# Moving the steps of the output chain and the empty places in the list that orders the ring of the third stage

## The chip, the cores and the metric

The kernel runs on one core of one Trainium2 chip. The metric is device time in microseconds (us), lower is better; the time stated for a kernel is the median of its runs. The engines are called TensorE (PE), VectorE (DVE), ScalarE (ACT), GpSimd (POOL) and SyncE (SP), as in the profile.

## The reference

Two cross-attentions and two feed-forward layers, each on a layer norm and added to x, for 4 batches of 256 rows of width 512. The context has 1601 rows per batch. The part that matters is the second attention (third stage of the kernel) and the last layer:

```python
def _L1_xattn_ref(latents, context, Wq, Wk, Wv, Wo):      # H, KV, HD = 16, 4, 96; G = 4
    hidden = jnp.concatenate([context, latents], axis=1)  # 1857 rows
    q = (latents @ Wq.T).reshape(b, q_len, H, HD)
    k = (hidden @ Wk.T).reshape(b, s_len, KV, HD)
    v = (hidden @ Wv.T).reshape(b, s_len, KV, HD)
...
    scores = jnp.einsum('bkgqd,bksd->bkgqs', q, k) * scale
    attn = jax.nn.softmax(scores.astype(jnp.float32), axis=-1).astype(q.dtype)
    out = jnp.einsum('bkgqs,bksd->bkgqd', attn, v)
...
    return out @ Wo.T
...
x = x + _L1_xattn_ref(_layernorm(x, axis=-1), ctx_4096, L1_xattn_Wq, ...)
x = x + _L1_ffn_ref(_layernorm(x, axis=-1), L1_ffn_W, L1_ffn_b, L1_ffn_A, L1_ffn_Bmat, L1_ffn_LiMEs)
```

## The kernel before

Three stages run one after the other. The first two make the keys, values and queries of the second attention and put them into DRAM. The third, `grouped_attention`, starts at about 1015 us of the span and is the only one that the change touches.

**Steps and tiles.** The third stage has 16 steps `s`, one for each batch and key head. A step covers 4 query heads x 256 rows = 1024 columns and goes over 15 key tiles `kt` of 128 keys (the last has 65). For each tile TensorE computes the scores (`scores`, lines 1502 to 1504, two halves of 512 columns, three products each, since every operand is split in a high and a low part), ScalarE takes the exponential twice (`probs`, lines 1604 and 1607), GpSimd subtracts the two to get the low part (line 1417), and TensorE multiplies with the values (`values`, lines 1522, 1523, 1525, two halves of three products). TensorE does the scores one tile ahead: in the loop over `kt` it does `scores(s, kt + 1)` and then `values(s, kt)`. The banks of the scores go round three by three.

**The ring.** Beside this, the step has a list of other work, `beside(s)`, whose entries are called places here and counted from 0. TensorE takes one place after the first half of the scores, one after the second, one after the first half of the values and one after the second: four a tile up to tile 11, two in tiles 12 and 13. `None` is an empty place. The entries are: 32 `max`, the products (line 1435) that give the maxima of the scores for the next step `s + 1`, each read by VectorE's reduction (line 1690); four `stacked`, nine products each (line 1458), which multiply the output of the step before, `s - 1`, with the output weights, read by VectorE (line 1698); in steps 5, 9 and 13 also the last layer of the batch that is complete (`turn`, `h`, `z`, `h8`, `dl`); and three entries that only VectorE acts on (`OWN`). For TensorE these three are empty places. The items share three banks (`RB = 3`): TensorE may write ring item n only when VectorE has read item n - 3. VectorE reads them in the order of the list, and does its own entries where they stand.

**The output chain.** When step `s` ends, its output and the sums of its exponentials have to be turned into rows, divided, stacked and multiplied with the output weights. This happens in step `s + 1`, through DRAM:
- ScalarE copies the output out (line 1652) and issues sums<-o (line 1611), right after the first tile's exponentials of the new step;
- VectorE inverts the sums: own entry `invert` (line 1720);
- ScalarE sends the inverted sums to DRAM, `send_parts` (line 1615), and spreads them over the partitions, `spread_parts` (line 1619), which waits for the sent values to land;
- VectorE multiplies: own entry `normal` (line 1724), which waits for the spread;
- ScalarE copies the product out, `send_o` (line 1623), and back in stacked form, `stack_o` (line 1628), and rounds it, `stacked_hi` (line 1635);
- VectorE subtracts the rounded part: own entry `low` (line 1728);
- TensorE can then do the `stacked` items; the first waits for both parts.

ScalarE does its five steps behind the exponentials of fixed tiles, and each of them waits, on ScalarE, for what it needs; the exponentials of the next tile stand behind it. The steps named with DMAs are issued from ScalarE's queue; SyncE's queue loads keys, queries, values and weights of later steps.

**Layer norm.** In steps 5, 9 and 13 VectorE starts with the layer norm of the batch that is complete, 19 small operations, between which `fill(1)` takes seven places of the list, one at a time.

Of the kernel before, what the change touches and what calls it, by code (L numbers as in the profile page):

```python
# [1193 lines left out]
def grouped_attention(nc, A, ident, negid, ps, ln, home, q_scr, k_scr, v_scr, x_scr, wo_scr, sum_scr, o_scr, w1T, out):  # L1194
# [16 lines left out]
    with ExitStack() as ctx:  # L1211
# [3 lines left out]
        def sem(name):  # L1215
            return ctx.enter_context(nc.semaphore(name))
# [62 lines left out]
        step, w_mix, mix_ones = sem("dve_step1"), sem("w_mixture"), sem("mixture_ones")  # L1279
# [6 lines left out]
        def bank(i, n=BANK):  # L1286
            return ps[:, i * BANK:i * BANK + n]
# [5 lines left out]
        def beside(s):  # L1293
            maxima = [("max", s + 1, i) for i in range(NI)] if s + 1 < S else []
            if s == 0:
                return [None] * 12 + maxima
            if s == S:
                return [("sum", s - 1, 0)] + [("out", s - 1, i) for i in range(TT * G)]
            e = (s - 1) // KV1 - 1 if s % KV1 == 1 else -1
            later = [("turn", e, 0), ("turn", e, 1), ("h", e, 0), ("h", e, 1), ("z", e, 0), ("h8", e, 0), ("dl", e, 0)] \  # L1300
                if e >= 0 else [None] * 7
            most = maxima or [None] * NI
            own = [(kind, s - 1, 0) for kind in ("invert", "normal", "low")]
            order = most[:6] + own[:1] + most[6:14] + later[:2] + own[1:2] + most[14:19] + later[2:3] + most[19:23] + later[3:4] + most[23:26] + later[4:6] + \
                most[26:28] + later[6:] + [None, None] + own[2:] + [None]
            for i in range(NO):
                order += [("stacked", s - 1, i), most[28 + i]]
            return order
# [10 lines left out]
        for s in range(S + 1):  # L1319
            for item in beside(s) + (last_batch() if s == S else []):  # L1320
                if item and item[0] not in OWN:
                    ring[item] = len(ring)
# [98 lines left out]
        def _(pe):  # L1421
            def ring_item(kind, a, i):
# [4 lines left out]
                if kind == "max":  # L1427
                    if i == 0:
                        pe.wait_ge(qh_in[a % 3], loads(a, 3))
                        pe.wait_ge(kh_in[a % 3], loads(a, 3))  # L1430
                        if a == 1:
                            pe.wait_ge(ones, 4)
                    j, ch = i // len(cuts), i % len(cuts)
                    k0, _, k = cuts[ch]
                    mm = pe.matmul(at[:, 0:k], qh[a % 3][0:HD1, j * P:(j + 1) * P], kh[a % 3][0:HD1, k0:k0 + k],  # L1435
                                   start=True, stop=True)
# [93 lines left out]
            for s in range(S):  # L1530
                if s == 1:
                    pe.wait_ge(w_small, 48)
                items = iter(beside(s))

                def fill():
                    item = next(items, None)
                    if item and item[0] not in OWN:
                        ring_item(*item)

                if s == 0:  # L1540
                    scores(0, 0, lambda: None)
                for kt in range(KT):
                    if kt + 1 < KT:
                        scores(s, kt + 1, fill)
                        fill()
                    elif s + 1 < S:
                        scores(s + 1, 0, lambda: None)
                    if s + 1 < S and kt == KT - 2:
                        max_rows(s + 1)
                    late = kt > KT - 4  # L1550
                    values(s, kt, (lambda: None) if late else fill)
                    if not late:
                        fill()
                assert next(items, None) is None
            for item in beside(S) + last_batch():
                ring_item(*item)
# [29 lines left out]
        def _(act):  # L1586
# [9 lines left out]
            def probs(s, kt):  # L1596
                n = s * KT + kt
                if n >= 2:
                    act.wait_ge(av_mm, n - 1)
                for half in range(2):  # L1600
                    src = bank((2 * n + half) % SB)[0:keys[kt], :]
                    cols = slice(half * BANK, (half + 1) * BANK)
                    act.wait_ge(s_mm, 2 * n + half + 1)
                    act.activation(ph[0:keys[kt], n % 2, cols], src, ACT.Exp, scale=S1).then_inc(phi, 1)  # L1604
                    if 2 * n + half >= 2:
                        act.wait_ge(plo, 2 * n + half - 1)
                    act.activation(pf[0:keys[kt], half, :], src, ACT.Exp, scale=S1).then_inc(exp_done, 1)  # L1607

            def send_sums(s):
                act.wait_ge(o_done, 2 * s + 2)  # L1610
                act.dma_start(sums[:, :], o[HD1:HD1 + 1, :].rearrange("o (j m) -> o j m", j=QT)).then_inc(sum_in, 16)
# [26 lines left out]
            for s in range(S):  # L1638
                for kt in range(KT):
                    if kt:  # L1640
                        probs(s, kt)
                    if s:
                        step = {2: send_parts, 3: spread_parts, 6: send_o, 7: stack_o, 9: stacked_hi}.get(kt)
                        if step:
                            step(s - 1)
                if s + 1 < S:
                    probs(s + 1, 0)
                act.wait_ge(av_mm, (s + 1) * KT)
                if s:
                    act.wait_ge(o_out, 16 * s)  # L1650
                for half in range(2):
                    act.copy(o[0:HD1 + 1, half * BANK:(half + 1) * BANK], bank(OB + half)[0:HD1 + 1, :]).then_inc(o_done, 1)  # L1652
                send_sums(s)
# [184 lines left out]
```

## Time and profile before

| | us |
|---|---|
| median of 3 runs | 1986.28 |
| lowest and highest run | 1984.8, 1987.23 |
| profiled execution | 1983.97 |
| its span | 1982.2 |
| TensorE busy | 1886.7 (95%) |
| VectorE busy | 1041.9 (53%) |
| ScalarE busy | 907.7 (46%) |
| GpSimd busy | 631.1 (32%) |

The rows are from one profiled execution; its own time is 1.8 us over its span. The busy share of TensorE is the mean over three stages. Products are pipelined: a row's duration is longer than the distance to the next row's start, so the time that TensorE loses is read from starts that lie further apart than their neighbours', and from the idle time in brackets at the end of a row, with what released it.

### The profile page before, as it was taken

Reading aid. Unit: us, or ns where it says so; the run is one execution under the profiler, and the core shown is the slowest. Engines: PE = TensorE matmul, PEld = TensorE weight load, DVE = VectorE, ACT = ScalarE, POOL = GpSimd, SP = SyncE. Lnnn points to the kernel's source line nnn. Section 1 sums busy time; section 2 is a strip of 40 time slices with the busy share of each in tenths; the row PEclk is TensorE's granted clock in tenths of the full one; section 3 lists DMA queues with packets and bytes.
Section 4 is the critical chain, followed back from the end, with each engine's and each line's share of the span. In section 5 each row is a group of like instructions: output and inputs, shape, how many; then the busy total and the mean of one; then the engine's idle time right before and its main releaser. Section 6 shows DMA issues by size and latency. Waiting matters only on the chain. (4 is left out here: it accounts for less than half of the span.)

```text
span 1982.2 us, 23779 instructions
## 1 busy us (share of the span) xinstructions
PE 1886.7 (95%) x8840; PEld 1348.1 (68%) x8840; DVE 1041.9 (53%) x2013; ACT 907.7 (46%) x1726; POOL 631.1 (32%) x504
## 2 busy tenths in 40 slices
PE   7999997999999999999899999999999999999997
PEld 6999894444556465555677777767777777767763
DVE  3464435676666765666535454464445455554414
ACT  3333331544344344334146566545655466645650
POOL 0000000000000000000037677657766577665760
PEclk9999995999999999999989999999999999999996
DMA  5978953000111020020186543335544145543101
GB/s 182 287 247 254 291 194 98 0 1 17 43 43 60 11 75 22 22 80 30 65 228 142 129 128 104 103 82 130 133 122 123 42 112 140 130 122 92 57 25 42
DMA packets 192953, 208.46 MB, mean 105 GB/s; under 512 B 87425, under 2 KB 157569, under 8 KB 192838
## 3 DMA queue, kind: packets, MB, share of 16 engines
q1 hardware_dynamic: 177124, 188.92, 33.6%
q10 hardware_dynamic: 15714, 18.03, 3.0%
q8 instruction: 70, 1.15, 0.2%
q14 instruction: 45, 0.37, 0.1%
HBM read 128.90 MB, written 77.94 MB: 104 GB/s over the span
## 5 line engine op out<-in xcount | busy, mean ns | idle before, releaser
L1417 POOL TENSOR_TENSOR pl<-pf,ph 128x512 fp32r<-128x512 f32 (+1 forms) x480 | 623.4, 1321 | 284.9 <-ACT pf L1607 283.9
L1604 ACT ACTIVATE ph<-ps 128x512 fp32r<-128x512 f32 (+1 forms) x480 | 288.1, 600 | 381.0 <-PE ps L1504 303.1
L1690 DVE TENSOR_REDUCE pm<-ps 128x1 f32<-128x464 f32 x480 | 299.3, 636 | 193.7 <-PE ps L1435 192.5
L1140 DVE TENSOR_REDUCE pm<-ps 128x1 f32<-128x400 f32 (+3 forms) x544 | 285.6, 573 | 92.0 <-PE ps L987 88.2
L1047 ACT ACTIVATE pr<-ps 128x512 f32<-128x512 f32 (+1 forms) x416 | 219.8, 600 | 197.4 <-PE ps L919 196.5
L1607 ACT ACTIVATE pf<-ps 128x512 f32<-128x512 f32 (+1 forms) x480 | 289.0, 602 | 5.0 <-POOL pl L1417 3.6
L1406 POOL MEMSET vh<- 128x30 f32 x1 | 0.2, 155 | 701.1 <-POOLq L684 701.1
L932 PE MATMUL ps<-pr,cv 128*64 128x512 f32 (+1 forms) x832 | 212.3, 626 | 0.0
L1525 PE MATMUL ps<-pl,vh 128*97 128x512 f32 (+1 forms) x480 | 190.7, 397 | 1.6 <-POOL pl L1417 0.8
L1522 PE MATMUL ps<-ph,vh 128*97 128x512 f32 (+1 forms) x480 | 191.5, 399 | 0.0
L1523 PE MATMUL ps<-ph,vl 128*97 128x512 f32 (+1 forms) x480 | 189.3, 394 | 0.0
L1435 PE MATMUL ps<-kh,qh 96*128 96x464 f32 x320 | 121.4, 380 | 11.8 <-DVE pm L1690 11.8
L1502 PE MATMUL ps<-qh,kh 104*128 104x512 f32 x300 | 122.6, 409 | 0.7 <-ACT pf L1607 0.6
L932 PEld LDWEIGHTS ps<-pr,cv 128*64 128x64 f32 (+1 forms) x832 | 52.2, 140 | 87.5 <-issue 61.5
L1525 PEld LDWEIGHTS ps<-pl,vh 128*97 128x97 f32 (+1 forms) x480 | 78.0, 162 | 42.2 <-POOL pl L1417 10.2
L987 PE MATMUL ps<-home,ast 96*128 96x400 f32 (+1 forms) x256 | 91.7, 421 | 6.3 <-DVE pm L1140 2.9
L901 POOL MEMSET home<- 96x1 f32 x1 | 0.1, 96 | 303.8 <-POOLq L158 303.8
L1523 PEld LDWEIGHTS ps<-ph,vl 128*97 128x97 f32 (+1 forms) x480 | 78.9, 164 | 24.4
L1522 PEld LDWEIGHTS ps<-ph,vh 128*97 128x97 f32 (+1 forms) x480 | 78.5, 163 | 22.9 <-issue 0.2
L987 PE MATMUL ps<-cst,ast 96*128 96x400 f32 (+1 forms) x256 | 84.3, 386 | 5.4 <-DVE pm L1140 3.7
L987 PEld LDWEIGHTS ps<-home,ast 96*128 96x128 f32 x256 | 49.9, 209 | 57.7 <-DVE pm L1140 28.6
L1435 PEld LDWEIGHTS ps<-kh,qh 96*128 96x128 f32 x320 | 60.1, 188 | 35.7 <-DVE pm L1690 18.8
(264 smaller groups left out, 3132.4 us busy)
## 6 DMA issues: line engine op xcount, KB each, us to landing
woT<-wo_turned SPq DMA_DIRECT2D x30, 768.0 KB, 6.1
v_scr<-vst SPq DMA_DIRECT2D x16, 1152.0 KB
cnat<-in_ctx_dram SPq DMA_DIRECT2D x16, 768.0 KB
q_scr<-qst SPq DMA_DIRECT2D x48, 256.0 KB, 2.5
vh<-v_scr SPq DMA_DIRECT2D x15, 672.0 KB
vl<-v_scr SPq DMA_DIRECT2D x15, 672.0 KB
home<-k_scr SPq DMA_DIRECT2D x14, 696.4 KB, 8.7
k_scr<-home SPq DMA_DIRECT2D x24, 384.0 KB, 7.4
```

The source lines that it names most:

```text
L932: mm = pe.matmul(bank(OB)[64 * half:64 * half + 64, :], cv[0:keys[kt], b % 2, kt, :], pr[0:keys[kt], n % NPR, half * BANK:(half + 1) * BAN ...
L987: mm = pe.matmul(out[:, 0:k], queries, keys_t, start=True, stop=True)
L1047: act.activation(pr[0:keys[kt], n % NPR, half * BANK:(half + 1) * BANK], bank((2 * n + half) % SB)[0:keys[kt], :], ACT.Exp, scale=S0).then ...
L1140: dve.reduce_max(pm[:, j, ch:ch + 1], src[:, 0:(cuts if s < S else next_cuts)[ch][1]], AX)\
L1417: pool.tensor_tensor(pl[0:m, n % 2, cols], pf[0:m, half, :], ph[0:m, n % 2, cols].bitcast(F32), ALU.subtract).then_inc(plo, 1)
L1435: mm = pe.matmul(at[:, 0:k], qh[a % 3][0:HD1, j * P:(j + 1) * P], kh[a % 3][0:HD1, k0:k0 + k], start=True, stop=True)
L1522: pe.matmul(out, vh[0:m, s % 2, kt, :], ph[0:m, n % 2, cols], start=(kt == 0), stop=False)
L1523: pe.matmul(out, vl[0:m, s % 2, kt, :], ph[0:m, n % 2, cols], start=False, stop=False)
L1525: mm = pe.matmul(out, vh[0:m, s % 2, kt, :], pl[0:m, n % 2, cols], start=False, stop=(kt == KT - 1))
L1604: act.activation(ph[0:keys[kt], n % 2, cols], src, ACT.Exp, scale=S1).then_inc(phi, 1)
L1607: act.activation(pf[0:keys[kt], half, :], src, ACT.Exp, scale=S1).then_inc(exp_done, 1)
L1690: ins = dve.reduce_max(pm[:, j, ch:ch + 1], at[:, 0:cuts[ch][1]], AX)
```

## The change

The list of steps 1 to 15 is written in another order, and ScalarE's five steps of the chain stand behind other tiles. The inversion goes from place 6 to 11, the multiplication from 17 to 23, the subtraction from 39 to 41, and the first stacked item from 41 to 42; the last item is at place 49 instead of 48. ScalarE's steps go from behind tiles 2, 3, 6, 7, 9 to behind tiles 4, 5, 7, 8, 10. One more empty place is in the list (four instead of three), and those that stood together ahead of and behind the subtraction now stand singly.

```diff
--- before.py
+++ after.py
@@ -1301,8 +1301,9 @@
                 if e >= 0 else [None] * 7
             most = maxima or [None] * NI
             own = [(kind, s - 1, 0) for kind in ("invert", "normal", "low")]
-            order = most[:6] + own[:1] + most[6:14] + later[:2] + own[1:2] + most[14:19] + later[2:3] + most[19:23] + later[3:4] + most[23:26] + later[4:6] + \
-                most[26:28] + later[6:] + [None, None] + own[2:] + [None]
+            order = most[:11] + own[:1] + most[11:13] + later[:2] + most[13:17] + [None] + most[17:19] + own[1:2] + [None] + \
+                later[2:3] + most[19:22] + [None] + most[22:24] + later[3:4] + most[24:26] + later[4:6] + most[26:28] + \
+                later[6:] + [None] + own[2:]
             for i in range(NO):
                 order += [("stacked", s - 1, i), most[28 + i]]
             return order
@@ -1640,7 +1641,7 @@
                     if kt:
                         probs(s, kt)
                     if s:
-                        step = {2: send_parts, 3: spread_parts, 6: send_o, 7: stack_o, 9: stacked_hi}.get(kt)
+                        step = {4: send_parts, 5: spread_parts, 7: send_o, 8: stack_o, 10: stacked_hi}.get(kt)
                         if step:
                             step(s - 1)
                 if s + 1 < S:
```

VectorE in a step without layer norm (the first of them), from the first maxima to the first stacked item; `pm` are maxima, `x3` and the like count equal rows. Before:

```order
L1690 TENSOR_REDUCE pm<-ps 128x1 x6
L1720 RECIPROCAL sums_inverted<-sums 8x128
L1690 TENSOR_REDUCE pm<-ps 128x1 x8
L1724 TENSOR_TENSOR o<-o,o_inverted 96x1024
L1690 TENSOR_REDUCE pm<-ps 128x1 x14
L1728 TENSOR_TENSOR o1sl<-o1s,o1sh 128x768
L1698 TENSOR_TENSOR x<-ps,x 128x256
```

After:

```order
L1691 TENSOR_REDUCE pm<-ps 128x1 x11
L1721 RECIPROCAL sums_inverted<-sums 8x128
L1691 TENSOR_REDUCE pm<-ps 128x1 x8
L1725 TENSOR_TENSOR o<-o,o_inverted 96x1024
L1691 TENSOR_REDUCE pm<-ps 128x1 x9
L1729 TENSOR_TENSOR o1sl<-o1s,o1sh 128x768
L1699 TENSOR_TENSOR x<-ps,x 128x256
```

The inversion stands behind eleven maxima instead of six, the multiplication behind 19 instead of 14; all 28 maxima still stand ahead of the subtraction.

TensorE at the place where the first stacked item stands, in tile 10 (the second half of the scores of tile 11, then the values of tile 10). Before:

```order
L1502 MATMUL ps<-qh,kh 128x512
L1503 MATMUL ps<-qh,kl 128x512
L1504 MATMUL ps<-ql,kh 128x512
L1458 MATMUL ps<-woT,o1sh 128x256 x6
L1458 MATMUL ps<-woT,o1sl 128x256 x3
L1522 MATMUL ps<-ph,vh 97x512
L1523 MATMUL ps<-ph,vl 97x512
L1525 MATMUL ps<-pl,vh 97x512
```

After:

```order
L1503 MATMUL ps<-qh,kh 128x512
L1504 MATMUL ps<-qh,kl 128x512
L1505 MATMUL ps<-ql,kh 128x512
L1523 MATMUL ps<-ph,vh 97x512
L1524 MATMUL ps<-ph,vl 97x512
L1526 MATMUL ps<-pl,vh 97x512
L1459 MATMUL ps<-woT,o1sh 128x256 x6
L1459 MATMUL ps<-woT,o1sl 128x256 x3
L1523 MATMUL ps<-ph,vh 97x512
L1524 MATMUL ps<-ph,vl 97x512
L1526 MATMUL ps<-pl,vh 97x512
```

The first stacked item (nine products) now comes behind the first half of the values instead of ahead of it, and the maximum that stood behind the first half stands behind the second.

VectorE at the end of the layer norm of step 5, from the last maximum ahead of xn. Before:

```order
L1690 TENSOR_REDUCE pm<-ps 128x1
L85 TENSOR_SCALAR xn<-x,ln_mv,ln_y 128x512
L1720 RECIPROCAL sums_inverted<-sums 8x128
L85 TENSOR_SCALAR xn<-x,ln_mv,ln_y 128x512
L1690 TENSOR_REDUCE pm<-ps 128x1 x8
```

After:

```order
L1691 TENSOR_REDUCE pm<-ps 128x1
L85 TENSOR_SCALAR xn<-x,ln_mv,ln_y 128x512
L1691 TENSOR_REDUCE pm<-ps 128x1
L85 TENSOR_SCALAR xn<-x,ln_mv,ln_y 128x512
L1691 TENSOR_REDUCE pm<-ps 128x1 x4
L1721 RECIPROCAL sums_inverted<-sums 8x128
L1691 TENSOR_REDUCE pm<-ps 128x1 x2
```

Between the two halves of xn stands a maximum instead of the inversion, which comes four maxima later.

## Rows read from the trace of the kernel before

**Rows 1.** Page, part 1: busy time, share of the span and instructions of each engine.

```profile
PE 1886.7 (95%) x8840; PEld 1348.1 (68%) x8840; DVE 1041.9 (53%) x2013; ACT 907.7 (46%) x1726; POOL 631.1 (32%) x504
```

**Rows 2.** Windows of eleven steps: stretch, us, busy by engine, granted clock, DMA share, GB/s.

```profile
1178.29:1233.23 54.94, 54.09 (x250) 41.37 (x250) 27.09 (x42) 32.98 (x63) 39.05 (x31) 1.00 0.47 120
...
1824.50:1877.72 53.22, 53.22 (x251) 41.57 (x249) 27.74 (x41) 32.73 (x63) 38.19 (x31) 1.00 0.32 82
sum 601.90, PE 592.17 PEld 456.25 DVE 299.47 ACT 362.53 POOL 428.96; mean PE 53.83 PEld 41.48 DVE 27.22 ACT 32.96 POOL 39.00
```

**Rows 3.** Timeline of TensorE, step 3: start, us, line, operation, idle before, releaser.

```profile
1177.68 0.37 PE L1435 MATMUL ps<-kh,qh 96*128 96x464 f32 x1
1177.89 0.39 PE L1502 MATMUL ps<-home 104*128 104x512 f32 x1
...
1186.33 0.40 PE L1525 MATMUL ps<-pl,vh 128*97 128x512 f32 x1
1187.17 0.47 PE L1435 MATMUL ps<-kh,qh 96*128 96x464 f32 x1 [0.44 <-DVE pm L1690]
...
1192.98 0.50 PE L1502 MATMUL ps<-home 104*128 104x512 f32 x1 [0.32 <-ACT pf L1607]
```

**Rows 4.** Timeline of VectorE: inversions of steps 3, 4 and 14, multiplication of step 3.

```profile
1185.68 0.94 DVE L1720 RECIPROCAL sums_inverted<-sums 8x128 f32<-8x128 f32 x1 [2.41 <-DMA sums<-o]
...
1194.63 1.99 DVE L1724 TENSOR_TENSOR o<-o,o_inverted 96x1024 f32<-96x1024 f32 x1 [2.69 <-DMA o_inverted<-sum_scr]
...
1241.83 0.94 DVE L1720 RECIPROCAL sums_inverted<-sums 8x128 f32<-8x128 f32 x1 [3.58 <-DMA sums<-o]
...
1830.54 0.94 DVE L1720 RECIPROCAL sums_inverted<-sums 8x128 f32<-8x128 f32 x1 [1.04 <-DMA sums<-o]
```

**Rows 5.** Timeline of ScalarE, step 3: its DMA issues and the exponential behind send.

```profile
1178.29 0.65 ACTq L1611 DMA_DIRECT2D sums<-o  x1
...
1186.65 0.28 ACTq L1615 DMA_DIRECT2D sum_scr<-sums_inverted  x1
1187.03 0.60 ACT L1604 ACTIVATE ph<-ps 128x512 fp32r<-128x512 f32 x1 [3.39 <-DVE sums_inverted L1720]
...
1191.42 0.32 ACTq L1619 DMA_DIRECT2D o_inverted<-sum_scr  x1
```

**Rows 6.** Windows of step 3 (DMA share next to last); then issue to landing of o1s<-o_scr.

```profile
1186.29:1188.29 2.00, 1.56 (x7) 0.91 (x6) 2.00 (x5) 1.26 (x3) 0.10 (x1) 1.00 1.23 261
1190.29:1192.29 2.00, 2.00 (x11) 1.49 (x9) 1.28 (x2) 0.45 (x1) 0.44 (x1) 1.00 0.06 12
...
DMA to landing us min/median/max: 2.8/3.0/3.1
```

**Rows 7.** Timelines of step 14, end of its chain: ScalarE, VectorE, GpSimd, TensorE; then line 1728.

```profile
1853.87 0.85 ACT L1635 CAST o1sh<-o1s 128x768 fp32r<-128x768 f32 x1
...
1854.95 1.51 DVE L1728 TENSOR_TENSOR o1sl<-o1s,o1sh 128x768 fp32r<-128x768 f32 x1
...
1853.10 2.55 POOL L1417 TENSOR_TENSOR pl<-pf,ph 128x512 fp32r<-128x512 f32 x2 [0.89 <-ACT pf L1607]
...
1856.98 0.40 PE L1502 MATMUL ps<-qh,kh 104*128 104x512 f32 x1
...
1858.39 0.87 PE L1458 MATMUL ps<-woT,o1sh 128*128 128x256 f32 x6
...
L1728 DVE TENSOR_TENSOR o1sl<-o1s,o1sh x15: 948/1514/1712, 1100.7 to 1903.5; 128x768 fp32r<-128x768 f32 x15
```

**Rows 8.** Timelines of step 15: VectorE's subtraction, TensorE at its tile 10.

```profile
1903.50 1.71 DVE L1728 TENSOR_TENSOR o1sl<-o1s,o1sh 128x768 fp32r<-128x768 f32 x1 [13.69 <-ACT o1sh L1635]
...
1905.31 0.40 PE L1502 MATMUL ps<-home 104*128 104x512 f32 x1
```

**Rows 9.** Timelines of step 5, start: VectorE, then TensorE.

```profile
1299.91 0.94 DVE L1720 RECIPROCAL sums_inverted<-sums 8x128 f32<-8x128 f32 x1
...
1301.82 0.48 PE L1435 MATMUL ps<-home 96*128 96x464 f32 x1 [1.18 <-DVE pm L1690]
```

## The prediction

> **What bounds the kernel now.** The page comes first: TensorE is busy 95% of the span, so what it waits is all there is to win [rows 1]. Next is the view of windows, cut from one issue of sums<-o to the next, one window per step. Eleven of the third stage's steps run the same instructions and none of the layer norm (1 to 4, 6 to 8, 10 to 12, 14). Together they last 601.90 us; the shortest, step 14, lasts 53.22 us with TensorE busy all through, at a granted clock of 1.00 like step 3 [rows 2]; the clock has nothing to give here. Step 14 is the floor: the eleven lose 601.90 - 11 x 53.22 = 16.5 us. The timelines of one step (step 3; t = 1178.29, the issue of sums<-o) say where it goes. I count in key tiles: a tile is 12 products at about 0.23 us plus 0.21 us for each maximum, 2.8 to 3.6 us [rows 3], and tile 0 begins three products before the first maximum, at 1176.99 = t - 1.3. A place then lies at t - 1.3, plus 2.8 us a whole tile, 0.7 us a half of scores or values, and 0.21 us a maximum ahead of it. Tile k's exponentials end about 2.9 us after tile k - 1 began (step 14's rounding follows tile 9's, 0.3 us before tile 9 [rows 7], and tile 8 with its two maxima takes 3.2 us).
>
> (a) VectorE reaches the inversion at its place 6 and waits for the sums until t + 7.4 [rows 4]. Meanwhile it reads no maximum. TensorE may only be three ring items ahead, and stands at its place 10: the product at 1187.17 could have begun at 1186.56, so 0.6 us is lost [rows 3]. Without the wait it would have come there at t + 8.3; less 0.94 for the inversion and 0.64 for the read behind it, sums that land after t + 6.6 cost TensorE time one for one. Step 14's landed at t + 6.0, step 4's at t + 8.6.
>
> (b) ScalarE's send behind tile 2 waits for the inversion until t + 8.4 (3.39 us idle), and its spread behind tile 3 waits for the sent values to land, until t + 13.1 [rows 5]. Exponentials stand behind both, and TensorE feels it at 1192.98 (idle 0.32 us, with its restart 0.6 us [rows 3]) and in the values products after it. The window of step 3 is 1.7 us over the floor [rows 2]; less 0.7 us for (a) with its restart, about 1 us is (b).
>
> **The change, part by part.** Products, exponentials and transfers stay the same in number; only places move.
>
> *Inversion, place 6 to 11.* VectorE now comes to it after maximum 10, which TensorE issues at t + 8.5 and which is read by t + 9.5. The sums of the eleven land between t + 6.0 and t + 8.6 [rows 4], so it no longer waits. If they came later, TensorE would stand only at place 17 (two empty places lie before it), at t + 14.2, and the limit moves from t + 6.6 to t + 12.5. Price now: 0.
>
> *Send behind tile 4, spread behind tile 5.* Send is issued around t + 12.2, inversion done by t + 10.5: no wait. In step 3 the sent values needed 4.8 us up to the spread [rows 5], in a stretch whose DMA share was 1.23; by t + 12 it is 0.06 [rows 6]. Even with 4.8 us the spread goes at t + 17.0, and tile 6's exponentials can begin only at about t + 17.3, once their scores are there. The cover is ScalarE's idle time, and it holds up to a landing about 5.1 us after the send. Price 0; if the cover were gone, (b) comes back.
>
> *Multiplication, place 17 to 23, and the two copies behind tiles 7 and 8.* The spread lands 3.2 us after its issue [rows 4, 5], by t + 20.2 at the latest; VectorE comes to place 23 at about t + 19.6 and needs 2.0 us. The next ring item that this can hold is at place 30, t + 25: covered. The copy out behind tile 7 is due at t + 22.3, just after. SyncE's load of the output weights waits for the last stacked item, which moves by one place (0.9 us); its need is a step away. GpSimd's queue is unchanged.
>
> *The end of the chain is where the change costs something.* Rounding moves from behind tile 9 to behind tile 10, one whole tile, but the first stacked product moves by one place only, 41 to 42. Step 14 gives the offsets [rows 7]: rounding starts at 1853.87, 0.3 us before tile 9's first product (tile 9 is twelve products and no maximum, 2.8 us, so it began at about 1854.2); the subtraction starts 1.08 us later and takes 1.51 us, so it ends 2.6 us after the rounding began. Before, that leaves 1858.39 - 1856.46 = 1.9 us of room. Now it ends at tile 10's start - 0.3 + 2.6 = + 2.3 us. Place 42 is after six score products (1.41 us, 1856.98 to 1858.39) and three of values (0.70 us): + 2.1 us. TensorE waits 0.2 us, and 0.1 us more for a cold start as behind other waits. Bounds: 0 (should rounding start a little sooner) and 0.9 us (what step 15 gives, below). I take 0.3 x 11 = 3.3 us, near step 14's row.
>
> The Trainium skill speaks against this place: "SBUF — State Buffer", section "SBUF: two separate sides", says that a VectorE operation with two SBUF inputs and a GpSimd one exclude each other for a whole instruction. The trace agrees in kind: the subtraction takes 1.51 us beside GpSimd and ends 0.8 us after GpSimd's pair at 1853.10 to 1855.65.
>
> *Step 15* has no maxima and shorter tiles. Its subtraction ended at 1905.21, level with tile 10's start at 1905.31 [rows 8]; rounding was 0.1 us after tile 9's start and not before it. One tile later the subtraction ends at tile 10 + 2.7 to 2.9 against TensorE at + 2.1: up to 0.9 us, of which part falls together with waits on GpSimd it has anyway. I take 0.5.
>
> *Layer-norm steps 5, 9, 13.* TensorE stands three times at their start because VectorE works through small operations; the third time ends at 1301.82 [rows 9]. There VectorE does the inversion (0.94 us) between the two halves of xn. Now maximum 6 stands there (0.6 us), so maxima come free earlier, while the two waits before it stay. Followed product by product, tile 3 begins about 0.5 us sooner. Bounds 0 and 1.3 us (that whole wait). 3 x 0.5 = 1.5 us. Behind that, h, z, h8 and dl only change places; the logits' item (place 39) is read before the subtraction.
>
> **Sum.** -16.5 (a and b) + 3.3 (stacked) + 0.5 (step 15) - 1.5 (layer norm) = -14.2 us. The profiled execution took 1983.97 us (span 1982.2); it would take 1969.8. It is 2.3 us under the median, so the median becomes 1986.28 - 14.2 = 1972.1 us.
>
> **The rivals.**
> 1. *The subtraction meets GpSimd later.* If the shift puts a further GpSimd subtraction in front (1.3 us instead of the partial 0.6), it takes 2.2 us and TensorE waits 0.7 us more in 12 steps: 8.4 us, 1980.5. Against it: rounding and GpSimd hang on the same exponentials, so the phase should be that of before, a median of 1.51 us over fifteen [rows 7]. The skill's section above gives this result if GpSimd is first in line.
> 2. *The inversion stops waiting but (b) stays.* If the sent values take over 5.1 us, exponentials are late again: about 1 us in 11 steps, 1983. Against it: the DMA share falls to 0.06 there. It is the case in which the change does half of what it says.
> 3. *Slower: the stacked copy arrives late.* From the copy in (behind tile 8) to rounding (behind tile 10) there are now 6.6 us, before 7.05. From a landing 8 us behind the issue each further us falls on TensorE, in 12 steps: the gain is eaten at 1.2 us each, and at 2 us each the time is 1972 + 24 = 1996. Against it: o1s<-o_scr lands within 3.1 us in all fifteen [rows 6].
> 4. *More than forecast.* No stacked wait and 1.3 us in each layer-norm step: 16.5 + 3.9 = 20.4, 1965.9.
>
> **How the numbers follow.** Forecast 0.67, rival 1 0.12, rival 2 0.09, rival 3 0.03, rival 4 0.04, and 0.05 for the change costing elsewhere what it brings. The range: down to 16.5 + 3.9 = 20.4, 1966; up to 16.5 - 11 x 0.9 - 0.9 = 5.7 of gain, 1980.6, so 1980. About 0.2% (4 us) is what a measurement of this kernel can tell from no change. Faster by more: forecast, rivals 1 and 4, and most of the edge around them, 0.88; same 0.08; slower 0.04.
>
> **What the profile after would show.** Right: windows of steps near 53.5 us; no idle of VectorE before the inversion; no idle of ScalarE behind send and spread; a new small idle of TensorE (or its weight load) before the stacked products, released by VectorE's o1sl, of 0.1 to 0.4 us; layer-norm steps about 0.5 us shorter. Wrong: maxima still waiting for VectorE behind place 10, values products waiting for GpSimd after the spread, or a subtraction of over 2 us.

## The result

| | median | lowest and highest |
|---|---|---|
| before, 6 runs | 1984.95 us | 1984.26, 1987.23 |
| changed, 6 runs | 1977.39 us | 1972.03, 1979.56 |

The ratio is 0.9958 with a 95% interval of 0.9944 to 0.9971: 7.6 us less by the medians. The prediction was 1972.1 us (14.2 us less), its range 1966 to 1980. The direction is right and the time lies in the range, but only about half of the forecast gain arrived, and 0.9928, the ratio that 14.2 us would be, is outside the interval. Where the other half went is the subject of what follows.

The profiled execution of the changed kernel took 1977.87 us (span 1976.1). Its page, part 1, TensorE at 96% now; it answers to [rows 1]:

```profile
PE 1888.5 (96%) x8840; PEld 1355.8 (69%) x8840; DVE 1044.4 (53%) x2013; ACT 907.8 (46%) x1726; POOL 632.2 (32%) x504
```

The windows from one issue of sums<-o to the next answer to [rows 2]. The columns are the stretch, its length, the busy time of the five engines, the granted clock, the DMA share and GB/s. First come two of the eleven plain steps (the steps without layer norm, 1 to 4, 6 to 8, 10 to 12 and 14) and the sum of all eleven, then steps 5, 9, 13 (layer norm) and step 15:

```profile
1072.78:1126.39 53.61, 53.52 (x251) 41.63 (x250) 27.32 (x42) 32.98 (x63) 39.06 (x31) 1.00 0.44 115
...
1179.96:1233.52 53.56, 53.44 (x250) 41.60 (x250) 27.30 (x42) 32.93 (x63) 39.09 (x31) 1.00 0.49 126
...
sum 589.52, PE 588.00 PEld 457.72 DVE 300.41 ACT 362.64 POOL 430.16; mean PE 53.45 PEld 41.61 DVE 27.31 ACT 32.97 POOL 39.11
...
1287.26:1356.41 69.15, 66.54 (x293) 48.38 (x292) 36.59 (x68) 33.27 (x63) 38.97 (x31) 0.98 0.35 92
1517.07:1587.67 70.60, 67.66 (x292) 49.22 (x292) 36.94 (x68) 33.24 (x63) 39.02 (x31) 0.95 0.35 91
1748.48:1817.65 69.17, 66.54 (x292) 48.40 (x292) 36.57 (x68) 33.17 (x63) 38.95 (x31) 0.98 0.35 93
1871.22:1918.61 47.39, 44.88 (x206) 33.00 (x204) 6.38 (x7) 31.05 (x59) 37.48 (x29) 1.00 0.08 26
```

The eleven plain steps took 589.52 us, 12.4 us less, each now within 53.50 to 53.74 us. The layer-norm steps took 208.92 us (before 206.55), 2.4 us more, and for the first time with a granted clock under 1.00. Step 15 took 47.39 us (46.61). From the first issue of sums<-o to the last the stage is 9.2 us shorter (845.83 against 855.06 us).

The timeline of VectorE in step 3, which answers to [rows 4]: inversion, multiplication and subtraction. The issue of sums<-o is now t = 1179.96.

```profile
1189.39 0.93 DVE L1721 RECIPROCAL sums_inverted<-sums 8x128 f32<-8x128 f32 x1
...
1199.49 1.21 DVE L1725 TENSOR_TENSOR o<-o,o_inverted 96x1024 f32<-96x1024 f32 x1
...
1213.06 1.71 DVE L1729 TENSOR_TENSOR o1sl<-o1s,o1sh 128x768 fp32r<-128x768 f32 x1 [0.40 <-ACT o1sh L1636]
```

The inversion starts at t + 9.4 with no idle time before it, and so does the multiplication, at t + 19.5. The timeline of ScalarE, which answers to [rows 5], with the exponential behind send (1191.15) and behind spread (1194.39):

```profile
1191.15 0.28 ACTq L1616 DMA_DIRECT2D sum_scr<-sums_inverted  x1
1191.25 0.61 ACT L1605 ACTIVATE ph<-ps 128x512 fp32r<-128x512 f32 x1
...
1194.39 0.32 ACTq L1620 DMA_DIRECT2D o_inverted<-sum_scr  x1
1194.50 0.61 ACT L1605 ACTIVATE ph<-ps 128x512 fp32r<-128x512 f32 x1
```

Neither exponential has an idle time in front: the two waits of the kernel before, (a) for the sums at the inversion and (b) at ScalarE's send and spread, are gone. What came instead is the wait at the first stacked product, on TensorE in step 2:

```profile
1160.79 0.40 PE L1526 MATMUL ps<-pl,vh 128*97 128x512 f32 x1
1161.34 0.95 PE L1459 MATMUL ps<-woT,o1sh 128*128 128x256 f32 x6
```

These starts lie 0.55 us apart instead of 0.23: 0.32 us. And this is what TensorE did at the start of step 5, which answers to [rows 9]:

```profile
1290.99 0.40 PE L1505 MATMUL ps<-ql,kh 96*128 96x512 f32 x1
1292.48 0.48 PE L1436 MATMUL ps<-home 96*128 96x464 f32 x1 [1.10 <-DVE pm L1691]
...
1293.27 0.40 PE L1526 MATMUL ps<-pl,vh 128*97 128x512 f32 x1
1295.18 0.48 PE L1436 MATMUL ps<-home 96*128 96x464 f32 x1 [1.52 <-DVE pm L1691]
1295.50 0.56 PE L1523 MATMUL ps<-ph,vh 128*97 128x512 f32 x1
1295.86 0.63 PE L1524 MATMUL ps<-ph,vl 128*97 128x512 f32 x1
1296.28 0.63 PE L1526 MATMUL ps<-pl,vh 128*97 128x512 f32 x1
...
1299.11 0.40 PE L1504 MATMUL ps<-qh,kl 96*128 96x512 f32 x1
1299.34 0.39 PE L1505 MATMUL ps<-ql,kh 96*128 96x512 f32 x1
```

Two waits for VectorE (products 1.49 and 1.91 us apart instead of 0.21 to 0.23), and from the second on the products start 0.42 us apart instead of 0.23: the granted clock is at the lower of its levels, 1.2 instead of 2.4 GHz, until about 1298.9, 3.4 us in all. In step 9 it is at that level for 6.8 us. The windows of 4 us around it say the same:

```profile
1291.26:1295.26 4.00, 1.39 (x6) 0.68 (x5) 3.83 (x8) 1.38 (x3) 2.97 (x3) 1.00 1.19 254
1295.26:1299.26 4.00, 4.00 (x11) 3.10 (x12) 3.79 (x11) 0.58 (x2) 0.00 (x0) 0.57 0.88 186
```

### The profile page after: what moved, and what is told of

Same layout as the page of the kernel before. It is cut to its first block and busy times, and to the rows that moved or that the text cites. A ratio compares the mean times of both kernels' runs of the same rounds, so it can differ in the third digit from the quotient of the medians.

```text
span 1976.1 us, 23779 instructions
## 1 busy us (share of the span) xinstructions
PE 1888.5 (96%) x8840; PEld 1355.8 (69%) x8840; DVE 1044.4 (53%) x2013; ACT 907.8 (46%) x1726; POOL 632.2 (32%) x504
## 5 line engine op out<-in xcount | busy, mean ns | idle before, releaser
L1691 DVE TENSOR_REDUCE pm<-ps 128x1 f32<-128x464 f32 x480 | 307.6, 642 | 258.5 <-PE ps L1436 256.2
L987 PEld LDWEIGHTS ps<-cst,ast 96*128 96x128 f32 x256 | 45.6, 192 | 54.6 <-DVE pm L1140 33.1
```

The costliest lines, as they stand in the source:

```text
L987: mm = pe.matmul(out[:, 0:k], queries, keys_t, start=True, stop=True)
L1691: ins = dve.reduce_max(pm[:, j, ch:ch + 1], at[:, 0:cuts[ch][1]], AX)
```

## The experiments

All are edits of the changed kernel (line numbers shift by a few). The kernels were timed beside the one before on the same chip; in the first group (four kernels) that one's median is 1983.29 us, in the second (four) 1984.68, in the third (three) 1986.19. Each profile was cut into steps as above. In the results "plain" is the sum of the eleven steps, "norm" that of steps 5, 9 and 13. The numbers in brackets behind a median are the ratio to the kernel before and its 95% interval.

**The changed kernel once more.**

> The changed kernel once more, on the same chip as the next three, to have its spread. Theory A (the eleven plain steps gain 12.4 us; the three layer-norm steps lose 2.4 us because TensorE's granted clock falls behind their second wait; step 15 loses 0.8 us): about 1977.4 us, plain steps 53.5 to 53.7 us, layer-norm steps 69.1 to 70.6 us, clock under 1.00 only in those three steps of the third stage. Theory B (the shortfall against the forecast is chance of one profile, such as the 3.5 us by which the third stage began later): layer-norm steps near 68.8 us in this profile, or a start of the third stage that scatters by some us.

1975.32 us (ratio 0.9957, 0.9941 to 0.9973); plain 589.64, norm 208.78 (69.15, 70.57, 69.06), step 15 47.35 us. The steps repeat to 0.1 us, the fall of the clock included. What doesn't repeat is what lies ahead: the third stage's first sums<-o is at 1069.02 us here and at 1072.78 us in the first profile of the same kernel. Over all profiles of this study it scatters between 1066.65 and 1073.08 us, before any changed instruction. So theory A holds for the steps, and theory B has its share: up to 6 us between single executions have nothing to do with the change, and no difference of 2 us between medians is settled by these runs; the steps' sums are.

**Layer-norm steps as before.** They get the old list and the old places of the five steps of the chain.

```diff
+            if e >= 0:
+                order = most[:6] + own[:1] + most[6:14] + later[:2] + own[1:2] + most[14:19] + later[2:3] + most[19:23] + later[3:4] + most[23:26] + later[4:6] + \
+                    most[26:28] + later[6:] + [None, None] + own[2:] + [None]
...
-                        step = {4: send_parts, 5: spread_parts, 7: send_o, 8: stack_o, 10: stacked_hi}.get(kt)
+                        moved = s % KV1 != 1 or s == 1
+                        step = ({4: send_parts, 5: spread_parts, 7: send_o, 8: stack_o, 10: stacked_hi} if moved else
+                                {2: send_parts, 3: spread_parts, 6: send_o, 7: stack_o, 9: stacked_hi}).get(kt)
```

> Steps 5, 9 and 13 take the old list and ScalarE's old places, all others the new. Theory A: the three layer-norm steps return to 68.7 to 69.0 us, the clock stays at 1.00, the eleven plain steps stay at 53.6 us; 2.4 us less than the changed kernel, about 1975 us. Theory B: no difference from the changed kernel within 1 us, about 1977.4 us.

1974.45 us (0.9953, 0.9934 to 0.9971); plain 589.53, norm 206.47 (68.70, 69.03, 68.74), clock 1.00 in all fifteen steps. The 2.3 us are back in the norm steps, as theory A has it; in the median (0.9 us under the kernel above) they can't be told from the scatter.

**Only place 6 empty in the layer-norm steps.** The inversion stays at 11, as changed.

```diff
+            if e >= 0:
+                order = most[:6] + [None] + most[6:10] + own[:1] + most[10:12] + later[:2] + most[12:19] + own[1:2] + [None] + \
+                    later[2:3] + most[19:22] + [None] + most[22:24] + later[3:4] + most[24:26] + later[4:6] + most[26:28] + \
+                    later[6:] + [None] + own[2:]
```

> Only in steps 5, 9 and 13, place 6 of the list is empty as it was for TensorE before the change, so that maximum 6 stands at place 7 again; the inversion stays at place 11. Theory A in its narrow form (the clock falls because maximum 6 moved one place ahead, which puts the second wait 0.8 us behind the first instead of 1.5 us): the clock stays at 1.00, layer-norm steps about 68.3 us as the prediction had it, about 4 us less than the changed kernel, 1973.5 us. Rival C (it falls because the inversion left the layer norm, wherever maximum 6 is): the clock falls as in the changed kernel, layer-norm steps 69.1 to 70.6 us, 1977.4 us.

1973.90 us (0.9948, 0.9928 to 0.9969); plain 589.60, norm 207.02 (68.89, 69.20, 68.93). TensorE's timeline at the start of step 5:

```profile
1287.53 0.40 PE L1509 MATMUL ps<-ql,kh 96*128 96x512 f32 x1
1289.03 0.47 PE L1440 MATMUL ps<-home 96*128 96x464 f32 x1 [1.10 <-DVE pm L1695]
...
1290.50 0.40 PE L1530 MATMUL ps<-pl,vh 128*97 128x512 f32 x1
1291.74 0.48 PE L1440 MATMUL ps<-home 96*128 96x464 f32 x1 [0.85 <-DVE pm L1695]
1292.06 0.39 PE L1507 MATMUL ps<-qh,kh 104*128 104x512 f32 x1
1292.29 0.39 PE L1508 MATMUL ps<-qh,kl 96*128 96x512 f32 x1
```

The windows of 4 us around it:

```profile
1287.80:1291.80 4.00, 2.05 (x9) 1.14 (x8) 3.83 (x8) 1.39 (x3) 2.99 (x3) 1.00 1.20 258
1291.80:1295.80 4.00, 3.37 (x12) 1.90 (x12) 3.79 (x10) 2.16 (x4) 1.63 (x2) 1.00 0.79 168
```

The first wait is the same (1287.53 to 1289.03). But behind the released maximum six products run before the second wait instead of three, the second is 1.24 us between starts instead of 1.91, and the products behind it follow 0.23 us apart. Clock 1.00 in all three steps: the narrow form of theory A holds, rival C is out. The change moved maximum 6 from place 7 to 6; VectorE starts the read that frees its bank at the same moment in both (7.2 us behind sums<-o), so TensorE only arrives earlier, waits longer, and has worked less since the last wait. The length was not as expected, 68.9 to 69.2 instead of 68.3 us: the third wait is back too (1.65 us between starts), since with an empty place ahead VectorE reads no maximum between the halves of xn.

**The inversion back at place 6.**

```diff
-            order = most[:11] + own[:1] + most[11:13] + later[:2] + most[13:17] + [None] + most[17:19] + own[1:2] + [None] + \
+            order = most[:6] + own[:1] + most[6:13] + later[:2] + most[13:17] + [None] + most[17:19] + own[1:2] + [None] + \
```

> The inversion alone goes back to place 6 (maxima 6 to 10 one place later each); ScalarE's steps and the rest stay as changed. By the prediction's step (a), sums that land after t + 6.6 cost TensorE time one for one: with the landings of the trace of before that is about 11 us over the eleven plain steps; the layer-norm steps return to the old order at their start and give back about 2.4 us: together about 1986 us. Rival D (ScalarE's send and spread made most of the loss, the inversion under 4 us): 1978 to 1980 us.

1980.00 us (0.9981, 0.9969 to 0.9993); plain 595.75, norm 207.02 (68.88, 69.27, 68.87). One of the eleven windows and their sum:

```profile
1125.98:1180.58 54.60, 53.67 (x251) 41.53 (x250) 26.91 (x42) 32.98 (x63) 39.09 (x31) 1.00 0.46 123
...
sum 595.75, PE 590.18 PEld 456.90 DVE 295.90 ACT 362.70 POOL 429.81; mean PE 53.65 PEld 41.54 DVE 26.90 ACT 32.97 POOL 39.07
```

VectorE's inversion in that step, from its timeline:

```profile
1133.68 0.94 DVE L1721 RECIPROCAL sums_inverted<-sums 8x128 f32<-8x128 f32 x1 [2.71 <-DMA sums<-o]
```

6.1 us in the plain steps instead of 11, 4.3 with the norm steps' gain taken off, 4.7 in the medians. The median is the 1980 of rival D, but not for its reason: it had the inversion's wait under 4 us. The rule of (a) holds, and the size was off because the sums land earlier here than in the kernel before. The eleven landed at t + 6.7, 7.7, 7.7, 7.1, 7.2, 7.7, 7.0, 6.9, 8.1, 7.2 and 5.7; what lies over t + 6.7 adds up to 6.2 us, against 6.1 to 6.2 measured (from 589.64 or 589.52). It holds step by step: step 11, at 8.1, is 1.4 us longer than in the changed kernel, step 2 (7.7) 1.0 us, steps 1 and 14 not at all. The limit is 6.7, where the prediction had 6.6. In the kernel before, with landings up to 8.6, the same rule gives 10.2 of the 16.5 us to (a) and leaves 6.3 to (b).

**Send and spread back as well,** behind tiles 2 and 3.

```diff
-            order = most[:11] + own[:1] + most[11:13] + later[:2] + most[13:17] + [None] + most[17:19] + own[1:2] + [None] + \
+            order = most[:6] + own[:1] + most[6:13] + later[:2] + most[13:17] + [None] + most[17:19] + own[1:2] + [None] + \
-                        step = {4: send_parts, 5: spread_parts, 7: send_o, 8: stack_o, 10: stacked_hi}.get(kt)
+                        step = {2: send_parts, 3: spread_parts, 7: send_o, 8: stack_o, 10: stacked_hi}.get(kt)
```

> Inversion back at place 6 (as in the kernel with that edit alone) and ScalarE's send and spread back behind tiles 2 and 3; multiplication, copies and rounding stay as changed. By the prediction's part (b) the exponentials behind send and spread are late: 0.5 to 1.1 us in each plain step on top of the inversion's wait, about 6 us over the kernel with the inversion alone at place 6 (1980.0), so 1986. Rival: ScalarE's waits lie in its idle time and cost nothing by themselves, the inversion's wait is all of it: 1980.

1982.87 us (0.9990, 0.9978 to 1.0002); plain 602.55, norm 206.80. The sum of the eleven windows:

```profile
sum 602.55, PE 593.44 PEld 455.51 DVE 296.01 ACT 363.23 POOL 429.84; mean PE 53.95 PEld 41.41 DVE 26.91 ACT 33.02 POOL 39.08
```

ScalarE's timeline in step 3, the exponentials behind send and spread:

```profile
1183.47 0.60 ACT L1605 ACTIVATE ph<-ps 128x512 fp32r<-128x512 f32 x1 [3.02 <-DVE sums_inverted L1721]
...
1188.86 0.60 ACT L1605 ACTIVATE ph<-ps 128x512 fp32r<-128x512 f32 x1 [3.32 <-DMA sum_scr<-sums_inverted]
```

6.8 us more in the plain steps than with the inversion alone at place 6, near the 6 expected; the rival (all of it the inversion's) is out. Later landings of the sums are hardly a part of it: by the inversions' starts they lie 6.3 us over t + 6.7 here, 6.2 in the kernel above. The loss isn't spread as expected: over the changed kernel, and with what lies over t + 6.7 taken off, it is nothing in steps 1 and 14 and 1.5 us in steps 3 and 7. With both undone and the wait at the stacked products left in, the plain steps are at 602.55 us, as before the change (601.90).

**Rounding behind tile 9.**

```diff
-                        step = {4: send_parts, 5: spread_parts, 7: send_o, 8: stack_o, 10: stacked_hi}.get(kt)
+                        step = {4: send_parts, 5: spread_parts, 7: send_o, 8: stack_o, 9: stacked_hi}.get(kt)
```

> Only ScalarE's rounding goes back behind tile 9 (the copy in stays behind tile 8), list as changed. By the prediction's last part of the chain, the wait of 0.3 us before the first stacked product of the eleven plain steps is the subtraction's alone: plain steps fall from 53.6 to about 53.25 us, step 15 from 47.4 to about 46.6 us, together 4 to 5 us under the changed kernel (1975.3 in the last comparison, so about 1971). The copy in lands 3.0 us behind its issue, and rounding stands about 3.4 us behind it. Rival: rounding now waits for that copy (an idle row of ScalarE before it), exponentials come late, and the plain steps stay at 53.6 us or more.

1971.06 us (0.9932, 0.9917 to 0.9948); plain 585.57, norm 210.01 (68.40, 71.29, 70.32), step 15 46.55 us. The windows: step 3, the sum of the eleven, step 5 and step 15:

```profile
1179.23:1232.45 53.22, 53.22 (x250) 41.70 (x250) 26.48 (x42) 32.97 (x63) 39.81 (x31) 1.00 0.49 126
...
sum 585.57, PE 585.57 PEld 458.64 DVE 291.24 ACT 363.03 POOL 437.91; mean PE 53.23 PEld 41.70 DVE 26.48 ACT 33.00 POOL 39.81
...
1285.83:1354.23 68.40, 65.78 (x293) 46.96 (x292) 36.37 (x68) 33.31 (x63) 39.07 (x31) 1.00 0.36 93
...
1868.36:1914.91 46.55, 44.59 (x206) 33.04 (x204) 6.65 (x7) 31.08 (x59) 37.43 (x29) 1.00 0.08 26
```

The view of the subtraction's line (durations least, median and most, in ns):

```profile
L1729 DVE TENSOR_TENSOR o1sl<-o1s,o1sh x15: 948/955/1674, 1105.4 to 1894.2; 128x768 fp32r<-128x768 f32 x15
```

The eleven lie at 53.2 us with TensorE busy through all of it (585.57 of 585.57 us): 4.0 us of waits at the stacked products are gone, and 0.8 us in step 15. This is the floor that the prediction read from step 14 of the kernel before, 11 x 53.22 = 585.4 us. No idle time stands before rounding. It starts 4.0 us behind the issue of the copy in (3.4 were expected; 3.0 in step 15), and the copy lands 2.9 to 4.2 us behind it. Step 5 shows the norm step of the changed list with the clock at 1.00 throughout: 68.40 us against 68.76 before. In steps 9 and 13 it fell again, at a higher price than in the changed kernel (71.29 and 70.32 us against 70.60 and 69.17).

**Fewer maxima under the layer norm.** Empty places 2, 5, 8 in steps 5, 9, 13.

```diff
+            if e >= 0:
+                order = most[:2] + [None] + most[2:4] + [None] + most[4:6] + [None] + most[6:8] + own[:1] + most[8:10] + \
+                    later[:2] + most[10:17] + own[1:2] + most[17:18] + later[2:3] + most[18:24] + later[3:4] + \
+                    most[24:26] + later[4:6] + most[26:28] + later[6:] + [None] + own[2:]
```

> Only steps 5, 9 and 13: empty places at 2, 5 and 8 of the list, so that TensorE offers fewer maxima while VectorE does the layer norm; the maxima left over fill the later empty places. Theory: the three waits at the start (3.6 us a step before the change) come from TensorE being three ring items ahead, so with fewer items they shrink to under 1.5 us a step, the clock stays at 1.00, layer-norm steps at about 66 to 67 us; 6 to 9 us under the changed kernel, about 1968 us. Rival: VectorE's small operations set the pace whatever is offered (the score products are behind exponentials anyway), layer-norm steps stay near 68.8 us, 1973 us.

1974.62 us (0.9949, 0.9936 to 0.9962); plain 589.53, norm 206.35 (67.58, 70.06, 68.71). Less than expected, and the norm steps' mean is the 68.8 us of the rival. One wait is left of three or two, of 2.5 us instead of under 1.5, and the clock fell behind it in steps 9 and 13; where it didn't, the step took 67.6 us. So fewer maxima do shorten the waits in all (2.5 us against 3.6 before the change), which the rival denied, but the fall of the clock takes the gain back in two of three steps. The expectation of under 1.5 us was wrong: an empty place between VectorE's slow operations (last section) saves it a read but lengthens the operation that follows. VectorE in step 5 of the same list, from the repetition further down:

```profile
1284.90 1.21 DVE L79 TENSOR_TENSOR ln_t<-ln_y 128x2 f32<-128x2 f32 x1
1286.14 1.19 DVE L80 SCALAR_TENSOR_TENSOR ln_u<-ln_t,ln_v 128x2 f32<-128x2 f32 x1
```

In the changed kernel a read of 0.56 us stood ahead of L79, which took 0.68 us; without the read it takes 1.21.

**Both,** rounding behind tile 9 and these places.

> The edits of the two kernels before together. If their causes are independent, the gains add: plain steps 53.25 us, layer-norm steps 66 to 67 us, about 1963 to 1965 us. If the layer-norm steps' copy in now holds up the rounding, less.

1965.01 us (0.9907, 0.9893 to 0.9922); plain 585.45, norm 204.84 (68.63, 67.50, 68.71), step 15 46.59 us. The gains add, as far as the fall of the clock lets one see, and the copy in doesn't hold up the rounding here; the norm steps missed the 66 to 67 us expected. Repeated in the last group:

> The fastest kernel so far (rounding behind tile 9, empty places 2, 5 and 8 in the layer-norm steps), once more beside the next two: about 1965 us; plain steps 53.2 us; layer-norm steps 67.5 us where the clock stays at 1.00, 68.6 to 70 us where it falls behind the single wait of 2.5 us.

1964.89 us (0.9906, 0.9891 to 0.9921); plain 585.51, norm 205.87 (68.61, 68.56, 68.70), the clock fallen in all three. TensorE in step 5, the one wait and the products after it:

```profile
1285.49 0.40 PE L1530 MATMUL ps<-pl,vh 128*97 128x512 f32 x1
1288.26 0.48 PE L1440 MATMUL ps<-home 96*128 96x464 f32 x1 [2.37 <-DVE pm L1695]
...
1289.32 0.63 PE L1507 MATMUL ps<-qh,kh 104*128 104x512 f32 x1
```

2.77 us between two starts, full pace for three products, then 0.43 us apart. In step 12 of this profile, as once in step 15 of the last kernel below (0.24 us), the copy in lands late enough to hold up the rounding:

```profile
1713.33 0.84 ACT L1640 CAST o1sh<-o1s 128x768 fp32r<-128x768 f32 x1 [0.56 <-DMA o1s<-o_scr]
```

The step took 53.15 us all the same; there is still room behind it.

**Three waits apart, with rounding behind tile 9.** The edits of the place-6 and the rounding kernel together.

> Place 6 empty in the layer-norm steps (three separate waits, as before the change) and rounding behind tile 9. Theory A (the clock falls with two waits close together and not with three apart): no stretch of the third stage's steps under a granted clock of 1.00, layer-norm steps 68.9 to 69.2 us each, plain steps 53.2 us; stage 3.5 + 1.9 us shorter than the changed kernel's, about 1969 us. Rival: with rounding behind tile 9 the clock falls in some layer-norm steps here too, as it did in two of three with the changed list.

1967.93 us (0.9916, 0.9902 to 0.9930); plain 585.48, norm 207.00 (68.88, 69.21, 68.91), clock 1.00 in every step. Theory A as expected, the rival is out.

**The waits cut up.** As the both-kernel, with other empty places:

```diff
-                order = most[:2] + [None] + most[2:4] + [None] + most[4:6] + [None] + most[6:8] + own[:1] + most[8:10] + \
+                order = most[:3] + [None] + most[3:4] + [None] + most[4:6] + [None] + own[:1] + most[6:10] + \
```

> As the first, but with empty places 3, 5, 8 and the inversion at 9 in the layer-norm steps, so that VectorE still reads a maximum between its slow small operations and TensorE's wait is cut into several short ones. Theory A: no single wait over 1.5 us, clock at 1.00 in all three steps, layer-norm steps about 67.0 to 67.5 us, about 1963 us. Rival: the waits come together again around maximum 7, the clock falls, 1966 us.

1968.17 us (0.9913, 0.9898 to 0.9929); plain 585.51, norm 208.60 (69.43, 69.90, 69.27). A miss: waits of 0.8 to 0.9 and 2.2 us in steps 5 and 13, of 2.0 and 0.6 us in step 9, together again around maximum 7 as the rival had it, and the clock fell in all three.

Over all profiles, by how TensorE waits at the start of a norm step:

| waits (us over the pace, start behind sums<-o) | steps | clock fell |
|---|---|---|
| 1.3 at 3.7; 1.0 to 1.3 at 6.7; 1.3 to 1.4 at 11 | 18 | 0 |
| 1.3 at 3.7; 1.7 to 2.0 at 6.0 | 9 | 8 |
| 2.5 at 5.1 | 9 | 7 |
| two, of 0.6 to 2.2, between 7.4 and 11.1 | 3 | 3 |

The other groups wait less in all than the first: 2.9 to 3.3, 2.5 and 2.6 to 3.1 us against 3.6 to 4.0 us.

## Why the prediction was right, and where it was not

**(a) and (b), right.** Undone one after the other they cost 6.1 and 6.8 us in the plain steps. The limit of (a) measured 6.7, one for one; the prediction's own terms, 8.3 - 0.94 - 0.64, give 6.7 too and not the 6.6 that it wrote. The forecast of -16.5 us to the floor is what the plain steps reach once the new wait is out of the way, 585.5 us. But 16.5 is the loss in the one trace of the kernel before. Undoing both parts brings back 13 us, since the sums landed later in that trace (10.2 us over the limit against 6.2 and 6.3). Whether that is the kernel's or that one execution's is not shown.

**Multiplication and copies, right.** Nothing waits there in the changed kernel. Some sizes were off without consequence: send goes at t + 11.2 and not 12.2, the multiplication takes 1.2 us and not 2.0, and from the copy in to rounding there are 7.2 us and not 6.6. The subtraction, not the DMAs, is last in the chain.

**The stacked wait, right in place and nearly in size.** 0.3 us a step was forecast, 0.37 was measured against the floor (589.52 - 585.42, over 11), and taking rounding one tile ahead removed it. The trace after differs in one term: the subtraction starts 0.9 us behind the rounding's start and takes 1.71 us, where step 14 had 1.08 and 1.51. The sum is the same 2.6 us: both times the subtraction ends 0.8 us after a GpSimd operation (last section), and that one's end lies 1.8 us behind the start of rounding before as after. Rival 1, a subtraction of 2.2 us, did not come about. Step 15: 0.8 us measured, 0.5 taken, bound 0.9.

**The layer-norm steps, wrong, and the main miss.** The step that failed reads "while the two waits before it stay". They did not. Maximum 6 moved one place ahead, so the second wait grew from 1.0 to 1.7 us (1.3 to 2.0 in step 9) and came after 0.8 instead of 1.5 us of work, and behind it the granted clock fell from 1.00 to 0.50 for 3.4 us in steps 5 and 13 and 6.8 in step 9. Forecast -1.5, measured +2.4: 3.9 us. The estimate without the clock was fair: where it happened not to fall, in one step of nine, that was 0.36 us shorter than before (0.5 forecast). The prediction had looked at the clock, found 1.00 in the rows, and wrote that "the clock has nothing to give here"; that it could be lost was not asked.

**The sum.** In the stage -12.4 + 0.8 + 2.4 = -9.2 us against -14.2. The difference of 5.0 us is 3.9 (norm), 0.8 (stacked wait) and 0.3 (step 15). In the profiled pair this adds up: the stage starts 3.5 us later, is 9.2 us shorter, and what follows it 0.4 us shorter, together -6.1 us as between the profiled times. The medians differ by 7.6 us, 1.6 us less than the stage. That this is the scatter ahead of the stage is likely, but not shown run by run; that the one trace of the kernel before has later landings than its other executions would do it too.

That the time still lies in the range is in part luck. Its upper end made room for 0.9 us of stacked wait a step, of which 0.37 came, and this room took in the layer-norm steps, whose own bounds were 0 to 1.3 us of gain. The chance for a cost elsewhere was put at 0.05, without naming one.

Rivals 2 and 3 did not occur. In the two profiles of the changed kernel neither send, spread nor rounding waits. In others with its plain steps the sent values land up to 4.3 us behind the send, so that spread goes up to 1.1 us later (step 3 of the kernel with rounding behind tile 9), and no exponential is late for it: the cover of 5.1 us was there and was needed in part. What would have put the forecast right was a rival that was not on the list.

## What to carry over

Moving work off a wait is sized well by windows cut at a repeated event and the shortest step as the floor; here it gave 585.4 us, and 585.5 were reached. Read what the moved entries leave behind: an entry one place earlier can reach the same release sooner, so that a wait gets longer and comes closer behind the one before it, and the price can then be the clock. And when a chain's last link moves by a tile and its consumer by a place, move the link back: with about 3 us for the copy (up to 4.6) and 4.0 us of room, rounding could stay, and with that and fewer maxima under the layer norm the kernel takes 1965 us (ratio 0.9907).

## What the runs showed of the hardware

The granted clock falls in the middle of a stage in which TensorE is nearly always busy, behind waits of 2.5 us and less, and not by the sum of the waits: in the table the steps with the most waiting kept 1.00. Nor every time: 8 of 9 and 7 of 9 with the same instructions. From t + 4 to t + 8 of step 5, ahead of the fall, TensorE is busy for 1.39 us in the changed kernel, and for 2.05 us in the one with place 6 empty, which keeps its clock. The cost is the products at 0.42 or 0.43 instead of 0.23 us until it rises: 0.8 us in step 5 (69.15 against 68.40), and by estimate 2.6 us in step 9 with rounding behind tile 9 (71.29 against 68.40 and the 0.3 us by which step 9 is longer than step 5 before the change). What decides it, these runs don't settle; they show four arrangements.

VectorE's operations on two elements a row take 0.16 or 1.2 us. In step 5 of the changed kernel, duration in the second column:

```profile
1293.06 1.20 DVE L80 SCALAR_TENSOR_TENSOR ln_u<-ln_t,ln_v 128x2 f32<-128x2 f32 x1
...
1295.23 0.16 DVE L80 SCALAR_TENSOR_TENSOR ln_u<-ln_t,ln_v 128x2 f32<-128x2 f32 x1
```

They stand beside GpSimd's subtractions, 1.26 us each (start, duration):

```profile
1289.20 5.04 POOL L1418 TENSOR_TENSOR pl<-pf,ph 128x512 fp32r<-128x512 f32 x4 [1.40 <-ACT pf L1608]
1299.84 1.29 POOL L1418 TENSOR_TENSOR pl<-pf,ph 128x512 fp32r<-128x512 f32 x1 [5.60 <-ACT pf L1608]
```

The slow ones run while GpSimd works, though not every small one is slow there: the 128x1 TENSOR_SCALAR at 1289.80 took 0.15 us. At 1294.24 GpSimd runs out of work until 1299.84, because TensorE's scores are late, and from there the same operation takes 0.16 us. The same holds for the subtraction of the output chain, 1.71 us in the changed kernel and 0.95 us with rounding behind tile 9. GpSimd in the changed kernel, around the subtraction shown above (1213.06):

```profile
1211.41 2.54 POOL L1418 TENSOR_TENSOR pl<-pf,ph 128x512 fp32r<-128x512 f32 x2 [0.66 <-ACT pf L1608]
```

With rounding behind tile 9, VectorE's timeline and then GpSimd's:

```profile
1211.85 0.95 DVE L1729 TENSOR_TENSOR o1sl<-o1s,o1sh 128x768 fp32r<-128x768 f32 x1
```

```profile
1210.68 5.77 POOL L1418 TENSOR_TENSOR pl<-pf,ph 128x512 fp32r<-128x512 f32 x4 [0.66 <-ACT pf L1608]
```

In the changed kernel the subtraction starts at 1213.06, 0.38 us into GpSimd's second operation (1211.41 + 1.27 = 1212.68), and ends 0.82 us after that one (1213.95). One tile earlier it starts 0.1 us before GpSimd's first operation ends (1210.68 + 1.27 = 1211.95), takes 0.95 us, and GpSimd's four last 5.77 us instead of 5.04. Both times the one that comes second waits until the other's operation is over. The Trainium skill, "SBUF — State Buffer", section "SBUF: two separate sides", says just that of a VectorE operation with two SBUF inputs and a GpSimd one that reads SBUF: an exclusive lock and not a share of bandwidth. The trace agrees; the subtraction and L80 both have two inputs.

That these operations make the layer norm long enough to hold up TensorE is read from the timeline; no run took GpSimd's work away from beside them.
